# Attention stage of a vision tower: token mixing moved to the second half of a unit, one unit earlier, and the normalisation moved beside the projection

## The reference, cut to what matters

```python
h = jnp.einsum('bhid,oi,od->bho', x, weighted_sum, weight)      # token mixing: 16 sequences x 512 tokens x 256
a = layernorm(h)                                                # x0 in the kernel
n = (a - mean(a)) * rsqrt(var(a) + 1e-5) * g1 + beta1           # nh, nl in the kernel
q, k = elu((n @ wq) @ proj) + 1, elu((n @ wk) @ proj) + 1       # "features"
v = n @ wv                                                      # "values"
# causal linear attention, 16 heads of 64:
kv = kv + k_t[:, None] * v_t[None, :];  ksum = ksum + k_t
out_t = (q_t @ kv) / (q_t @ ksum + 1e-6)
a = a + out @ wo                                                # "project"
# then the MLP of this layer, and the routed experts with a shared one
```

## Time and profile before

| | |
|---|---|
| median of 3 runs | 2818.04 us (2816.8 to 2821.98) |
| the profiled execution: its own time | 2821.95 us |
| its span, first to last instruction | 2820.2 us |
| its mean granted TensorE clock | 0.945 |
| busy share: TensorE, VectorE, ScalarE, GpSimd | 86%, 70%, 52%, 56% |
| attention's units, in the span | from about 62 to about 1666 us |

### The profile page before, as it was taken

How to read it: one execution, slowest core, us unless ns; L and a number is a source line. 1 busy time by engine, 2 the same in 40 slices (tenths; PEclk the granted TensorE clock), 3 DMA queues, 4 the chain that set the end, 5 groups by cost and what they waited for, 6 DMA issues and landing times. The chain is left out here.

```text
span 2820.2 us, 61193 instructions
## 1 busy us (share of the span) xinstructions
PE 2421.0 (86%) x22832; PEld 1747.7 (62%) x22832; DVE 1960.4 (70%) x4174; ACT 1471.1 (52%) x2731; POOL 1585.0 (56%) x1548
## 2 busy tenths in 40 slices
PE   4899999999999999999999957998988889886564
PEld 3678777777878777787777743444444444443453
DVE  3667767777777777777777753877877687785442
ACT  3656656666666666656666634444444434432232
POOL 1555555656555565655566532556655665666566
PEclk8989999999999999999999978999999999998787
DMA  4212111111211111111110011111211211100576
GB/s 142 62 35 62 55 39 59 55 43 55 63 54 43 39 35 43 35 43 35 43 39 28 17 57 53 58 46 57 74 52 46 79 51 39 44 8 16 120 136 98
DMA packets 115060, 152.21 MB, mean 54 GB/s; under 512 B 16537, under 2 KB 75917, under 8 KB 114768
## 3 DMA queue, kind: packets, MB, share of 16 engines
q1 hardware_dynamic: 88880, 124.46, 14.1%
q0 software_dynamic: 23808, 21.74, 4.3%
q10 hardware_dynamic: 2080, 2.10, 0.2%
HBM read 81.71 MB, written 90.96 MB: 61 GB/s over the span
## 5 line engine op out<-in xcount | busy, mean ns | idle before, releaser
L943 POOL TENSOR_TENSOR qkl<-fz,qkh 128x512 f16<-128x512 f32 x256 | 297.2, 1161 | 283.9 <-DVE qkh L842 283.9
L514 PE MATMUL pF<-nh,qk_h 128*128 128x256 f16 x1024 | 288.0, 281 | 62.3 <-DVE vl L848 57.2
L955 POOL TENSOR_TENSOR ol<-on,oh 128x256 f16<-128x256 f32 x256 | 188.5, 736 | 208.3 <-ACT oh L779 208.3
L1797 POOL DMA_INDIRECT slot_dram<-xt,slot_u x256 | 257.7, 1007 | 75.7 <-issue 75.2
L516 PE MATMUL pF<-nl,qk_h 128*128 128x256 f16 x1024 | 287.8, 281 | 0.0
L515 PE MATMUL pF<-nh,qk_l 128*128 128x256 f16 x1024 | 287.7, 281 | 0.0
L763 ACT ACTIVATE ot<-pT 128x512 f16<-128x512 f16 x256 | 149.8, 585 | 184.3 <-PE pT L673 184.3
L756 ACT ACTIVATE sh<-sm 128x512 f16<-128x512 f32 x256 | 159.5, 623 | 106.1 <-DVE sm L865 106.1
L962 POOL TENSOR_TENSOR kvl<-kvacc,kvh 128x260 f16<-128x260 f32 x192 | 157.1, 818 | 91.7 <-ACT kvh L787 89.9
L889 DVE TENSOR_SCALAR dn<-pO 128x4 f32<-128x4 f32 x256 | 40.3, 157 | 235.1 <-PE pO L516 235.0
L839 DVE SCALAR_TENSOR_TENSOR fz<-pF,ez 128x512 f32<-128x512 f32 x256 | 174.8, 683 | 34.5 <-ACT ez L739 33.0
(11 more groups left out here) (315 smaller groups left out, 8779.7 us busy)
## 6 DMA issues: line engine op xcount, KB each, us to landing
xs<-in_x SPq DMA_DIRECT2D x128, 256.0 KB, 2.7
slot_dram<-blank SPq DMA_DIRECT2D x8, 1360.0 KB, 6.9
xg<-slot_dram SPq DMA_DIRECT2D x40, 272.0 KB, 3.5
h_dram<-hT SPq DMA_DIRECT2D x32, 256.0 KB, 2.2
x_dram<-x SPq DMA_DIRECT2D x32, 256.0 KB, 2.2
at_dram<-at SPq DMA_DIRECT2D x32, 256.0 KB, 2.2
x0b<-x_dram SPq DMA_DIRECT2D x16, 512.0 KB, 4.0
atb<-at_dram SPq DMA_DIRECT2D x16, 512.0 KB, 5.0
```

The costliest lines, as they stand in the source:

```text
L514: pe.matmul(out, wh, mh, start=first, stop=False, skip_group_check=True)
L943: nc.gpsimd.tensor_tensor(qkl[:, pair:pair + 2, cols], fz[:, n % 2, :, :], qkh[:, pair:pair + 2, cols], ALU.subtract).then_inc(fl_ready, 1)
L955: nc.gpsimd.tensor_tensor(ol[:, n % 2, :], on[:, n % 2, :, :].rearrange("p a b -> p (a b)"), oh[:, n % 2, :], ALU.subtract).then_inc(ol_re ...
L1797: nc.gpsimd.indirect_dma_start(io["slot_dram"], bass.IndirectOffsetOnAxis(slot_u[:, c, k:k + 1], 0), xt[:, i % 2, c, :], None, bounds_chec ...
```

## The change

`mix` now works on the unit three ahead and stands at the ends of slots 4 to 7, with `h` behind the last. The parts of the normalisation of the unit two ahead move to the first half: `mean` and `centre` to the end of slot 0; `var` and `rstd` into the middle of slot 1, ahead of f2; `x0` and `normed` to the very start of slot 2, ahead of the projection's matmuls in the common order (which on VectorE is ahead of `outputs` of slot 2). The first split for a unit stands at the end of slot 3. Ahead of the first unit, (1, 0) is mixed as well, and the normalisation of (0, 1) is one block in slot 4. SyncE's queue follows: `x0` of two ahead, attention of the unit before, four loads of the unit four ahead, `hT` of three ahead.

```diff
-            def norm(u, s):
-                if s < XS:
-                    step("mix", u, s)
-                    if s < XS - 1:
-                        step("split", u, s + 1)
-                    else:
-                        step("h", u)
-                elif s == 5:
-                    step("x0", u)
-            def norm_early(u, s):
-                if s == 4:
-                    step("mean", u)
-                    step("centre", u)
-                elif s == 5:
-                    step("var", u)
-                    step("rstd", u)
-                elif s == 6:
-                    step("normed", u)
+            def mixed(u, k):
+                step("mix", u, k)
+                if k < XS - 1:
+                    step("split", u, k + 1)
+                else:
+                    step("h", u)
+            def normed(u):
+                step("mean", u)
+                step("centre", u)
+                step("var", u)
+                step("rstd", u)
+                step("x0", u)
+                step("normed", u)
...
-                if mix:
-                    step("split", after(u, 2), 0)
+                ahead, far = after(u, 2), after(u, 3)
...
+                    if s == 2 and real(ahead):
+                        step("x0", ahead)
+                        step("normed", ahead)
                     for what in early:
                         use(u, *what)
                     step("outputs", i, c, g)
...
                     step("outputs_split", i, c, g)
+                    if s == 1 and real(ahead):
+                        step("var", ahead)
+                        step("rstd", ahead)
                     for what in late:
                         use(u, *what)
...
-                    if mix:
-                        norm_early(after(u, 2), s)
-                        norm(after(u, 2), s)
+                    if s == 0 and real(ahead):
+                        step("mean", ahead)
+                        step("centre", ahead)
+                    if s == 3 and real(far):
+                        step("split", far, 0)
+                    if s >= 4 and real(far):
+                        mixed(far, s - 4)
                     for what in late:
                         finish(u, *what[:2])
...
-                norm_early((0, 1), s)
-                norm((0, 1), s)
+                if s < XS:
+                    mixed((0, 1), s)
+                elif s == 4:
+                    normed((0, 1))
+            step("split", (1, 0), 0)
+            for k in range(XS):
+                mixed((1, 0), k)
```

More of the change, by code:

```diff
@@ L365, in dense, with unit @@
                 return slots
-            def unit(u, start=False, mix=True, last=False):
+            def unit(u, start=False, last=False):
                 i, h = u
                 slots = dense(start, last)
-                if mix:
-                    step("split", after(u, 2), 0)
+                ahead, far = after(u, 2), after(u, 3)
                 for s in range(8):
@@ L415, in run @@
             step("split", (0, 0), 0)
-            for s in range(8):
-                norm_early((0, 0), s)
-                norm((0, 0), s)
+            for k in range(XS):
+                mixed((0, 0), k)
+            normed((0, 0))
             step("split", (0, 1), 0)
@@ L434, in run @@
                 unit((i, 1))
-            unit((SEQS - 1, 0), mix=False)
-            unit((SEQS - 1, 1), mix=False, last=True)
+            unit((SEQS - 1, 0))
+            unit((SEQS - 1, 1), last=True)
             step("turn", SEQS - 1, CH - 1, 2)
@@ L469, in clear_slots, with unit @@
                 sp.dma_start(rows, blank[:, :].unsqueeze(1).broadcast_to([P, TILES, ROW])).then_inc(slots_cleared, 16)
-            def unit(u, start=False, load_more=True, mix=True):
+            def unit(u, start=False):
                 if u[1] == 1 and u[0] < EXPERTS:
                     clear_slots(u[0])
-                if load_more:
-                    load(after(u, 3), 0)
-                    load(after(u, 3), 1)
+                if after(u, 2)[0] < SEQS:
+                    store_x0(after(u, 2))
                 if not start:
                     store_attention(after(u, -1))
-                if load_more:
-                    load(after(u, 3), 2)
-                    load(after(u, 3), 3)
-                if mix:
-                    store_rows(after(u, 2))
+                if after(u, 4)[0] < SEQS:
+                    for k in range(XS):
+                        load(after(u, 4), k)
+                if after(u, 3)[0] < SEQS:
+                    store_h(after(u, 3))
             for u in ((0, 0), (0, 1)):
@@ L489, in _ @@
             sp.dma_start(w2_w[:, :, :], io["w2"].rearrange("(t p) n -> p t n", p=P)).then_inc(mlp_loaded, 16)
-            store_rows((0, 0))
+            store_h((0, 0))
+            store_x0((0, 0))
             for k in range(XS):
                 load((1, 0), k)
-            store_rows((0, 1))
+            store_h((0, 1))
+            store_x0((0, 1))
+            for k in range(XS):
+                load((1, 1), k)
+            store_h((1, 0))
             unit((0, 0), start=True)
             unit((0, 1))
-            for i in range(1, SEQS - 2):
+            for i in range(1, SEQS):
                 unit((i, 0))
                 unit((i, 1))
-            unit((SEQS - 2, 0))
-            unit((SEQS - 2, 1), load_more=False)
-            unit((SEQS - 1, 0), load_more=False, mix=False)
-            unit((SEQS - 1, 1), load_more=False, mix=False)
             store_attention((SEQS - 1, 1))
```

5 lines of the change are left out of this document (4 added, 1 removed).

## The result

The changed kernel takes 2746.98 us (median of 4 runs, 2745.51 to 2749.88), the kernel before 2817.47 us on the same chip. The ratio is 0.9748, 95% interval 0.9731 to 0.9765: 70.5 us faster. The forecast was 2759, so the direction holds and the gain is 12 us larger than the sum said.

What follows compares the result with a forecast made beforehand. TensorE's issue rate was taken to bound the attention, plus waits from VectorE's crowded second half. Gains of 119 + 7 us less 57 + 9.5 given back made 59 us: from the 2818.04 median to 2759, range 2728 to 2800.

Steps and rivals of the forecast that it cites:

- Removed, second half: Slots 4 to 7: mixes in, normalisation out; TensorE's waits of 94 to 95 us and 24 us of clock go, together 119.
- VectorE's lateness at slot 2: Normalisation at slot 2's start delays `dn`: 2.0 us late for h = 0, 1.5 for h = 1.
- VectorE's lateness from there to slot 4: Slot 2 to slot 4, h = 0: v0 waits 0.5 us, and 1.2 us of lateness reach slot 3's `sl`.
- The term of 3.8 us a pair: New TensorE waits for a pair of units: 2.2 + 1.2 + 0.4 us, times 15 = 57 us.
- Slot 4's own 1.0 us: TensorE waits 1.0 us for `sl` before slot 4's `outputs` in every unit, since mixes no longer cover it.
- The mix's wait for `xl`: Slot 4: the first mix stands right behind its split, which comes late in slot 3; 0.15 us a unit.
- Prologue and end: Serial normalisation of (0, 1) 5 us, later splits of (1, 0) 2.5, unit (14, 1) without cover 2: together 9.5 us lost.
- the rims: Around each TensorE wait matmuls start about 0.15 us later than the idle says; three waits less a pair gain 7 us.
- C: Rival: the block fits beside slot 2's projection, only slot 4's 1.0 us waits remain; 2733 us, chance 0.14.
- A: The forecast as summed, with a remaining wait at slot 4's `outputs`: 2742 to 2778 us, chance 0.50.
- B: Rival: first half takes back most, by GpSimd contention (35 us) or clock falling after new waits (24 us); 2783 to 2812, chance 0.22.
- E: Rival, slower: extra block lateness passes through `at`, `kvt`, `fz`, `sl` one for one to slot 4; decides at 2.0 us a unit, chance 0.09.

Runs made afterwards that it cites:

- late block: The changed kernel with `x0` back at the end of slot 5 and `tn`, `nh`, `nl` back in slot 6, mixes left in slots 4 to 7: ratio 0.9924.
- thin block: The changed kernel with `x0`, `tn` and `nl` computed for 8 of 256 columns from the third unit on, for timing only: ratio 0.9692.
- three more instructions: The changed kernel with three extra VectorE instructions like `x0`, into a spare tile, ahead of `x0` in slot 2 from the third unit on: ratio 0.9958.
- both moves: Mixes in slots 3, 5, 6, 7 with spread prologue (0.9624), altered: mixes in slots 3, 4, 5, 7, 0.9672; or splits issued earlier, 0.9663.

## Why the prediction came out as it did

**Removed, second half: right.** The 57.2 us for `vl` went, with the satellites for `kt` and `fz`, and the clock shows 1.00 in each 300 us from 400 to 1300 us. That the mixes alone don't earn it is what the late block shows: with the cover alone some 20 of the 70 us are left. Whether the block moved out alone would earn it isn't shown. The prediction had booked the gain without saying which part earns it. On the clock it was wrong in two details. It read 2.9 us for a slow f0, the time from 793.40 to the start at 796.34, which holds idle time; the 12 matmuls take 2.5, 1.2 more than at the full clock. And it said that the clock dropped only after the longest wait: f0 was slow after ten of the fifteen longest, and also after one of 1.74 us, at 141.99.

**VectorE's lateness at slot 2: right.** The timeline of VectorE, unit with h = 0; p started at 685.34:

```profile
688.99 0.43 DVE L856 CAST qkh<-fz 128x512 f16<-128x512 f32 x1
689.33 0.69 DVE L826 TENSOR_TENSOR x<-xc,r 128x512 f32<-128x512 f32 x1
690.12 1.59 DVE L837 SCALAR_TENSOR_TENSOR tn<-x,g,r 128x256 f32<-128x256 f32 x2
692.02 0.88 DVE L843 SCALAR_TENSOR_TENSOR nl<-tn,b,nh 128x256 f16<-128x256 f32 x2 [0.31 <-ACT nh L738]
692.82 0.16 DVE L903 TENSOR_SCALAR dn<-pO 128x4 f32<-128x4 f32 x1
...
693.56 0.68 DVE L870 TENSOR_SCALAR at<-pF 128x512 f32<-128x512 f32 x1
...
694.76 0.42 DVE L925 TENSOR_TENSOR kvt<-pKV,block_mask 128x260 f32<-128x260 f32 x1
...
699.59 0.69 DVE L862 SCALAR_TENSOR_TENSOR vl<-pF,vh 128x512 f16<-128x512 f32 x1 [0.37 <-ACT vh L759]
...
700.86 0.68 DVE L886 TENSOR_TENSOR sl<-sm,sh 128x512 f16<-128x512 f32 x1
```

The cast ends 4.1 us after p's start (predicted 4.1), the block takes 3.5 us to the start of `dn` (3.7), and `dn` starts 7.5 us after p, 1.7 late against 5.8 (2.0). For h = 1 it starts 7.21 us after p in nearly all units, 1.1 late where I had 1.5.

**VectorE's lateness from there to slot 4: the step that failed.** I had 1.2 of the 2.0 us arrive at `sl` of slot 3 and add to the 1.0 us of the earlier trace rows, and 0.5 us of wait at v0. Measured, v0 starts without a wait, just as `at` ends (TensorE, p and v0):

```profile
685.34 0.27 PE L528 MATMUL pF<-ot,wo_h 128*128 128x256 f16 x1
...
694.30 0.39 PE L528 MATMUL pF<-wv_h,nh 128*128 128x512 f16 x1
```

`kvt` starts 9.42 us after p, where unit (15, 0) had it at 8.56: 0.9 late. `sl` starts 15.52 after p against 15.10: 0.4 late. The lateness shrinks because there were more gaps than the one ahead of `kvt` that I used: VectorE waits 0.37 us for `vh` even here, and the cast of f3 took 0.55 us where unit (15, 0) had 0.97. "From there VectorE works without a pause" was wrong. TensorE itself reaches the place 0.4 us later too, so the idle time stays 1.0. The term of 3.8 us a pair measured 2.3. The thin block settles it: with 0.9 us less lateness in each unit slot 4's wait is the same, and a pair is 0.4 us shorter.

**Slot 4's own 1.0 us: right**, read from the one unit of the trace of before that had no mixing at all. The kernel with a mix in slot 3 removes it and gains 31 us, as expected from 2 us times 15.

**The mix's wait for `xl`:** predicted 0.15 us a unit at the first mix, in slot 4. That one doesn't wait; the fourth, in slot 7, does, 0.22 us once a pair.

**Prologue and end: the size of two parts off, the sum right in this trace, by luck.** First scores came at 110.02 us against 92.98, 17.0 later, 5.24 of it moved matmuls: 11.8 lost, where I had 7.5. The main waits are

```profile
86.94 1.13 PE L557 MATMUL pM<-sq,ones 128*128 128x256 f32 x4 [2.93 <-ACT sq L714]
93.67 0.39 PE L528 MATMUL pF<-nh,qk_h 128*128 128x256 f16 x1 [2.98 <-DVE fz L853]
103.13 0.37 PE L528 MATMUL pM<-xh,tok_h 128*128 128x256 f16 x1 [2.53 <-POOL xl L951]
```

By the first projection 2.8 us of it are made good (14.2 later, 9.0 of it loss), and the end costs nothing. 9.5 were booked. But the second trace of the same kernel has the first scores at 107.36 and the first projection at 167.67 us, which is 9.1 and 4.7 us of loss; TensorE's granted clock from 60 to 150 us was 0.92 there and 0.87 here. Of the kernel before there is only one trace. So these losses are known to some 4 us, and that 9.0 meets 9.5 proves nothing.

**The sum.** Predicted for a pair: 119 / 15 + 7 / 15 - 3.8 = 4.6 us; measured 5.4. The new waits were put 1.5 us too high (3.8 for 2.3), the removed waits, the clock and the rims 0.2 or 0.3 each, which takes back nearly half of it. Over 14 pairs the difference is 11.6 us. The slow first pairs of the kernel before add 4.7 that I had not seen (the two falls of the clock at 197.5 and 397.5 us; why they came later than the others, no run asked), and the last unit gives 0.3 where I had 2.6. Up to the last projection: 64.4 + 11.6 + 4.7 + 0.3 - 9.0 = 72.0, the 72.2 of these two traces, against 59.5.

**An agreement by chance.** I had written that TensorE's waits from 100 to 1600 us would be near 57 us, and they are 55.6. But I meant steady waits, and those are 31 to 34; the other 22 stand at the two ends of the stage, which the prediction did not count into that window.

**The rivals.** C (2733, the waits are the 1.0 us alone) was nearest in mechanism, though the block doesn't fit wholly beside the projection; the time lies in A's range of 2742 to 2778, 12 us below its sum. B did not happen: the block meets one `qkl`, and the bill is small. In the rows above `tn` took 1.59 us; in the kernel with three more instructions, where `qkl` was done before `tn` began, 0.88. GpSimd's `qkl` took 1.54 us instead of 1.15. Together 0.71 + 0.39 = 1.10 us, about one `qkl`, shared between the two engines; my 3.7 from averaged rows already held VectorE's part. The Trainium skill (SBUF — State Buffer, SBUF: two separate sides) says that the loser blocks for the other's whole instruction; the sum of the two delays agrees with that, but its use here, 4.1 us for the block, was above the 3.5 measured. GpSimd bore 0.39 us of it, and the block without `qkl` takes 2.77 us (1099.57 to 1102.34 in the kernel with three more), not 3.0. E named a true risk, and its rate was right: beyond what the change has, a microsecond of lateness costs 0.8 to 1.0 us. But it goes through `at` at v0 and `ot` at `keys`, not through `sl`. With 2.05 us more the kernel is still 0.4% under the kernel before; by an estimate from that, at one for one, the turn lies near 2.4 us (2.05, and 12 us over 30 units), not at 2.0.

## What to carry to other kernels

Moving work out from under a wait moves the cover of the places it came from; look for the unit or iteration that already lacks that work, since its trace shows the wait that the change will make everywhere. Late work on an in-order engine is absorbed by every gap behind it, small ones too, so walk the whole row of instructions to the consumer before adding lateness to a wait; and look at every consumer on the way, because once the gaps are used up the first of them pays nearly one for one. A slow clock behind a wait may stand where another wait would be: compare the places where it fell with those where it didn't before giving it a price. And when the last wait is half a microsecond, a move may only change its name, as both moves did here.

## What the runs showed of the hardware

- VectorE beside GpSimd, both reading SBUF: the pair of `nl` took 0.88 us in slot 2 and 2.67 in slot 6 beside `sl` and `xl`; `kvacc` 0.43 and 1.31; `sl` 0.69 and 1.15; `x0` 0.717 on average in slot 2 against 0.945 in slot 5. GpSimd's own instructions stretched less: `sl` beside `nl` from 1.15 to 1.34 us, `qkl` beside `x0` to 1.54. In slot 6 of the late block VectorE lost most; in slot 2 it lost 0.71 us and GpSimd 0.39.
- The granted clock was 0.81 in the five microseconds about one 2.07 us wait and 1.00 about another of the same length, at 595.77 (1.00 from 585 to 605 us). In the steady units of the changed kernels it was 1.00 about every wait of 1.3 us or less whose windows were read, also with three more instructions, where waits of 1.14 and 0.75 us end at 1102.46 and 1103.82 (window of that kernel, columns as in the earlier trace rows; the next five microseconds show 1.00 as well):

```profile
1098.00:1103.00 5.00, 3.86 (x56) 3.26 (x54) 4.52 (x10) 1.39 (x3) 0.49 (x1) 1.00 0.15 52
```
